# Attention's output products in three 16-bit terms, with low parts made on VectorE, and the second key copy read from 16-bit data

## What is computed

```python
q = (x @ w_q).reshape(b, s, h, -1).transpose(0, 2, 1, 3)
kv = x @ w_kv
...
q = _l2norm(q) * jnp.exp(scale)
k = _l2norm(k)
sim = jnp.einsum('bhid,bhjd->bhij', q, k)
attn = jax.nn.softmax(sim, axis=-1)
out = jnp.einsum('bhij,bhjd->bhid', attn, v)
out = out.transpose(0, 2, 1, 3).reshape(b, s, h * out.shape[-1])
return out @ w_out + b_out
```

## Time and profile before

| | us |
|---|---|
| median of 3 runs (1051.28 to 1055.02) | 1051.43 |
| the profiled execution, its own time | 1044.7 |
| its span, first to last instruction | 1042.9 |
| TensorE busy / VectorE busy / ScalarE busy / GpSimd busy | 911.9 / 732.2 / 768.9 / 503.0 |
| first scores start | 35.0 |
| last output product starts | 631.5 |

### The profile page before, as it was taken

How to read it: one execution, slowest core, us unless ns; L and a number is a source line. 1 busy time by engine, 2 the same in 40 slices (tenths; PEclk the granted TensorE clock), 3 DMA queues, 4 the chain that set the end, 5 groups by cost and what they waited for, 6 DMA issues and landing times. The chain is left out here.

```text
span 1042.9 us, 34710 instructions
## 1 busy us (share of the span) xinstructions
PE 911.9 (87%) x13676; PEld 856.1 (82%) x13676; DVE 732.2 (70%) x1432; ACT 768.9 (74%) x1275; POOL 503.0 (48%) x384
## 2 busy tenths in 40 slices
PE   4789999999999999999999997989969589899930
PEld 2678998998999989888889987989958479899830
DVE  6699989888988988888998974424549769400202
ACT  5689998998988999988889865445465366697831
POOL 5465655555554654644778800323327180052423
PEclk8799999999999999999999998999989689899965
DMA  8400000000000000000001020713111012023111
GB/s 256 130 2 3 23 3 23 2 3 22 3 3 22 3 3 23 3 3 23 9 8 37 13 63 7 231 55 91 45 29 31 1 36 64 16 72 98 57 57 43
DMA packets 43563, 42.13 MB, mean 40 GB/s; under 512 B 5648, under 2 KB 37392, under 8 KB 43408
## 3 DMA queue, kind: packets, MB, share of 16 engines
q1 hardware_dynamic: 39312, 31.51, 10.1%
q0 software_dynamic: 4096, 8.40, 2.6%
HBM read 25.60 MB, written 14.29 MB: 38 GB/s over the span
## 5 line engine op out<-in xcount | busy, mean ns | idle before, releaser
L688 ACT ACTIVATE Pr<-SC,nesc,esc 128x1024 f32<-128x1024 f32 x256 | 310.0, 1211 | 33.2 <-PE SC L505 22.9
L804 DVE TENSOR_TENSOR Pl<-Pr 128x1024 f16<-128x1024 f32 x224 | 293.2, 1326 | 39.7 <-ACT Pr L688 38.1
L504 PE MATMUL SC<-QK 128*128 128x256 f16 x1024 | 238.6, 273 | 1.0 <-ACT QK L670 1.0
L505 PE MATMUL SC<-QK 128*128 128x256 f16 x1024 | 238.6, 273 | 0.0
L530 PE MATMUL OP<-V,Pr 128*128 128x65 f16 x2048 | 214.4, 192 | 6.3 <-DVE Ob L827 6.2
L532 PE MATMUL OP<-V,Pr 128*128 128x64 f16 x2048 | 215.3, 195 | 0.0
L534 PE MATMUL OP<-V,Pl 128*128 128x65 f16 x2048 | 214.1, 191 | 0.0
L530 PEld LDWEIGHTS OP<-V,Pr 128*128 128x128 bf16 x2048 | 191.0, 97 | 13.4 <-issue 9.2
L532 PEld LDWEIGHTS OP<-V,Pr 128*128 128x128 bf16 x2048 | 190.0, 97 | 2.6
L534 PEld LDWEIGHTS OP<-V,Pl 128*128 128x128 f16 x2048 | 190.7, 99 | 0.0
L1055 POOL TENSOR_TENSOR stk<-nrm,stk 128x512 f16<-128x512 f32 x64 | 75.1, 1173 | 139.8 <-DVE stk L786 139.8
(11 more groups left out here) (224 smaller groups left out, 2168.2 us busy)
## 6 DMA issues: line engine op xcount, KB each, us to landing
ys<-yb SPq DMA_DIRECT2D x92, 64.0 KB, 1.5
w_or_rows<-xs SPq DMA_DIRECT2D x12, 384.0 KB, 4.2
wst<-in_up SPq DMA_DIRECT2D x8, 512.0 KB, 3.5
xs<-zero SPq DMA_DIRECT2D x2, 1472.0 KB, 13.4
scratch<-in_up SPq DMA_DIRECT2D x4, 576.0 KB, 4.5
wd<-in_wd SPq DMA_DIRECT2D x4, 576.0 KB, 5.8
wd<-in_wd SPq DMA_DIRECT2D x4, 512.0 KB
QK<-in_wqkv SPq DMA_DIRECT2D x4, 384.0 KB, 7.5
```

The source lines that it names most:

```text
L504: eng.matmul(out, QK[:, b, 1, key:key + P], rhs, start=True, stop=False)
L505: mm = eng.matmul(out, QK[:, b, 2, key:key + P], rhs, start=False, stop=True)
L688: eng.activation(Pr[:, n % PB, :, :], SC[s % 2][:, :, :], ACT.Exp, bias=nesc[:, hd:hd + 1], scale=esc[:, hd:hd + 1]).then_inc(s_exps, 1)
L804: eng.tensor_tensor(Pl[:, n % PB, :, :].rearrange("p a b -> p (a b)"), pr, high(pr)[:, 1::2], ALU.subtract).then_inc(s_low_probs, 1)
```

## The change

It touches the output products, the output weights and the second key copy.

- `out_product` has three 16-bit matmuls instead of one 32-bit: the upper halves of `OT` (read as bf16 in place) with the high and with the low part of the weights, and the low part of `OT` with the high part of the weights. They add up in PSUM. It waits for `s_out_low` instead of `s_out_turned_read`.
- The low part of `OT` is a new subtraction on VectorE, `low_out`, 128 x 256 elements a unit, 64 in all, into a buffer `OTl` of two units. `low_slot` puts it two slots before its product: slots 7, 10, 13, 16, 23, 25, 27 and 29, behind that slot's `low_probs` and ahead of an `add_out` of the same slot. It waits for the copy of `OT` and for the product two units before, whose place in `OTl` it takes.
- The weights are loaded into `OT`'s memory and split once, in slots 16 and 18 of pass 0, on VectorE (`split_out_weights`): a cast to `wo_hi` and a subtraction to `wo_lo`. TensorE's wait for the load is gone; ScalarE's first copy into `OT` waits for the split, and each copy waits for the product of its place one pass before.
- `copy_keys` reads the 16-bit keys that `high_parts` has just written, instead of the 32-bit ones, and so waits for `s_qk_high` of its own group.

```diff
+SPLIT_WO_AT = (16, 18)
...
+def low_slot(u):
+
+    return OUT_AT[u] - 2
...
-        wo = sb("wo", [P, H // 2 * D], F32)
+        wo_hi = sb("wo_hi", [P, H // 2 * D], F16)
+        wo_lo = sb("wo_lo", [P, H // 2 * D], F16)
...
+        OTl = sb("OTl", [P, 2, 2 * P], F16)
+        wo = OT[:, 0:H // 4, :, :].rearrange("p u r c -> p (u r c)")
...
             def out_product(i, u):
 
-                wait(eng, s_out_turned_read, 8 * i + u + 1)
+                wait(eng, s_out_low, 8 * i + u + 1)
                 for r in range(2):
                     pair = (2 * i + u // 4) % TB
-                    mm = eng.matmul(out_bank(i, u)[:, P * r:P * r + P], OT[:, u, r, :],
-                                    wo[:, D * pair:D * pair + D], start=True, stop=True)
+                    out = out_bank(i, u)[:, P * r:P * r + P]
+                    hi, lo = high(OT[:, u, r, :])[:, 1::2], OTl[:, u % 2, P * r:P * r + P]
+                    wh, wl = wo_hi[:, D * pair:D * pair + D], wo_lo[:, D * pair:D * pair + D]
+                    eng.matmul(out, hi, wh, start=True, stop=False)
+                    eng.matmul(out, hi, wl, start=False, stop=False)
+                    mm = eng.matmul(out, lo, wh, start=False, stop=True)
                 mm.then_inc(s_out_product, 1)
...
-            eng.wait_ge(s_loaded["wo"], 16)
             eng.wait_ge(s_squares, PJ)
...
                 wait(eng, s_out_turned, 8 * i + u + 1)
+                if (i, u) == (0, 0):
+                    eng.wait_ge(s_wo_low, 1)
+                wait(eng, s_out_product, 8 * (i - 1) + u + 1)
                 eng.activation(OT[:, u, :, :], M1[:, 0:2 * P].rearrange("p (r c) -> p r c", r=2), ACT.Copy).then_inc(
                     s_out_turned_read, 1)
...
             def copy_keys(h, hb, g):
-                G, b = 4 * h + g, g % 2
+                G = 4 * h + g
                 wait(eng, s_turned, 8 * (h - 1) + 2 * g + 2)
-                eng.tensor_copy(stk[:, g, :, 4 * DH:5 * DH], nrm[:, b, :, 1, :]).then_inc(s_k_copied, 1)
+                wait(eng, s_qk_high, G + 1)
+                eng.tensor_copy(stk[:, g, :, 4 * DH:5 * DH], stk[:, g, :, 2 * DH:3 * DH]).then_inc(s_k_copied, 1)
...
+            def split_out_weights(s):
+
+                if s == SPLIT_WO_AT[0]:
+                    eng.wait_ge(s_loaded["wo"], 16)
+                    eng.tensor_copy(wo_hi[:, :], wo).then_inc(s_wo_high, 1)
+                if s == SPLIT_WO_AT[1]:
+                    eng.wait_ge(s_wo_high, 1)
+                    eng.tensor_tensor(wo_lo[:, :], wo, wo_hi[:, :], ALU.subtract).then_inc(s_wo_low, 1)
+
+            def low_out(i, u):
+
+                wait(eng, s_out_turned_read, 8 * i + u + 1)
+                wait(eng, s_out_product, 8 * i + u - 1)
+                o = OT[:, u, :, :].rearrange("p r c -> p (r c)")
+                eng.tensor_tensor(OTl[:, u % 2, :], o, high(o)[:, 1::2], ALU.subtract).then_inc(s_out_low, 1)
...
+                    split_out_weights(s)
+                if (x := out_unit(s, low_slot)) and exists(i, x[0]):
+                    low_out(i - x[0], x[1])
                 if (x := out_unit(s, out_slot)) and exists(i, x[0]):
```

More of the change, by code:

```diff
@@ L323, in attention @@
         s_k_copied = sem("s_k_copied")
+        s_wo_high = sem("s_wo_high")
+        s_wo_low = sem("s_wo_low")
+        s_out_low = sem("s_out_low")
         s_qk_low = sem("s_qk_low")
@@ L429, in _ @@
                     eng.dma_start(scl[:, :], io["scale"].partition_broadcast(P)).then_inc(s_loaded["scl"], 16)
-            eng.dma_start(wo[:, :], io["wout"]).then_inc(s_loaded["wo"], 16)
+            eng.dma_start(wo, io["wout"]).then_inc(s_loaded["wo"], 16)
             eng.dma_start(t["x"][:, :, :], io["x"].rearrange("(t p) d -> p t d", p=P)).then_inc(s_loaded["x"], 16)
```

## The result

The changed kernel takes **1112.45 us** (median of 4 runs, 1110.78 to 1114.36) against 1052.35 for the kernel before beside it: a ratio of 1.0571, interval 1.0550 to 1.0592. The forecast was 1067 with a range of 1055 to 1079: the sign was right, the size was missed by 45 us. The profiled execution took 1112.4 us, its span 1110.7.

A forecast was written before the change was run, and what follows sets the result against it. TensorE bounds by shares, with VectorE a second bound in slots 4 to 14 and 20 to 30. Passes lose 12.8 us and the tail 3.3, together 16.1, or 1.5% on the median 1051.43: 1067 us, range 1055 to 1079.

The forecast's parts named there:

- the copy should come at 0.04: Key copy on VectorE: starts 0.04 us after the cast ends, ahead of GpSimd's subtraction at 0.08; 0.06 us more per group.
- the rival: Key copy falls behind GpSimd's subtraction and waits 1.2 us, about 52 us on top: 1120 us; chance 0.06.
- TensorE's part: Output products: six 16-bit matmuls take 0.33 us, saving 0.19 us per unit, 0.11 in two units of eight.
- Its rival: TensorE decides and low parts are hidden: seven passes save 1.36 us each, 9.5 in all, 1042 us; chance 0.07.
- The low part: VectorE's 256-element subtraction per unit: 0.41 us until the result, 0.33 in VectorE's queue.
- First half: Pass 3, slots 4 to 20: TensorE waits on low parts, slot 15's product 1.51 us late; half loses 1.13 us.
- Second half: Pass 3: no loss in slot 25, slot 29's product delayed 1.23 us by its addition, savings 0.19 + 0.11; net 0.93 us lost.
- Passes 1 to 4: Attention's passes 1 to 4: each loses 2.06 us, 8.2 together.
- The split: Output weights' cast and subtraction (0.7 and 1.2 us) in pass 0, slots 16 and 18, where VectorE idles: loss taken as 0.
- Pass 5: ScalarE scales eight rows more and bounds more of the first half: half of a pass's loss, 1.2 us.
- The tail: Eight products after the last scores: units 1 to 4 wait for additions, 1.4 us a unit instead of 0.62; 3.3 us lost.
- The free wait: Waiting on the neighbour costs nothing: key copy saves 0.07 us per group instead of losing 0.06, 1061 us; chance 0.15.

The follow-up runs named there:

- with one wait: Changed kernel without the key copy's wait for the turned keys of the head before, leaving only the wait for the cast: 1073.35 us, 1.0192 to before.
- the run with early low parts: Changed kernel with the old 32-bit key copy, low parts of turned outputs taken in slots 0 to 3 and 16 to 19, four buffers: 1064.85 us.
- the best version: Changed kernel with old key copy, four low-part buffers, low parts in slots 0 to 3 and at the ends of slots 18 and 19: 1055.31 us, 1.0032.
- the next run: Old key copy, low parts in slots 0 to 3, 18 and 19, plus the weight split put before pass 0's first exponential: 1057.19 us, 1.0038.

## Why the prediction was wrong, point by point

**The step that failed** is "the copy should come at 0.04". I took the 0.04 from the earlier trace rows, where an instruction's wait for its neighbour stands in the instruction itself. The new wait was written last, became an instruction of its own, and the copy comes at 0.10, in all 60 groups of the slot loop between 0.102 and 0.104; GpSimd comes at 0.08 in 59 of them. With the wait in the copy itself it comes at 0.034, as I had read. 0.02 us decided over 39. The diff showed both waits and their order; I priced the added wait by its neighbour's end and did not ask where it stands.

**The chance.** I had the rival, its place and the two rows that it rested on. 0.06 for it was too little: the lead was 0.04 us, without a row for two waits, and the price 52 us by its own sum.

**The rival's size.** "About 1 us x 4 x 13 = 52 on top": a group holds VectorE 0.81 us longer (2.55 against 1.73 with one wait). Taken for all 60 groups, as pass 0 has them too, that makes 49, of which 39 reached the time. Pass 0, left out there, lost 4.7 of them (76.8 against 72.1).

The Trainium skill has this rule, and I did not weigh it: "SBUF — State Buffer", section "Who interferes with whom", says that VectorE's copies in two-port modes, and its instructions with two inputs from SBUF, share a pair of ports with GpSimd, that whoever issues first holds it for the whole instruction while "the other fully blocks", and that sums along the row take no part in it on this chip. The traces agree: a copy of 0.23 us takes 1.22 and ends 0.08 after GpSimd, a low part of 0.41 takes 1.95 and ends 0.28 after it, and the sum at 280.26 (GpSimd behind the copy) takes 0.68 beside GpSimd's subtraction as without it. In one point the traces are narrower: GpSimd's power of eight elements (1.63 us) does not hold VectorE. In the changed kernel 46 of VectorE's low probabilities run wholly beside it and take 1.19 to 1.23 us, as when GpSimd idles.

**TensorE's part** was right: 0.33 us for the six matmuls (in the run with early low parts a product starts at 285.88 and the next transposes at 286.22). Its rival, that TensorE decides and 9.5 us are saved, did not come about even with the low parts out of the full stretches of VectorE's queue: there 0.3 us a pass show.

**The low part**: 0.41 was right for the median (0.417), not for the mean: 0.52 with one wait, as 14 of 64 take over 0.6. In pass 3 those are the ones of slots 16 and 27 (0.88 and 0.87), which end 0.28 after GpSimd's subtraction for the values.

**First half**, forecast 1.13: with one wait 1.31 (36.69 against 35.38), and TensorE reaches slot 15's product 1.50 us late, where the sum said 1.51. The wait of 0.8 us in slot 12 is 0.6 there, but most of it stands before attention's products (0.43 at 286.04) and only 0.09 before the output product. **Second half**, forecast 0.93: 1.30. In slot 25, "no loss", the product is 0.5 later; in slot 29 it waits 1.29 us instead of 0.27, 1.0 more against the 1.23 worked out. TensorE, with one wait:

```profile
296.20 0.22 PE L565 MATMUL M<-wo_hi,OT 128*128 128x128 f16 x1 [0.57 <-DVE OTl L863]
...
331.08 0.22 PE L565 MATMUL M<-wo_hi,OT 128*128 128x128 f16 x1 [1.29 <-DVE x L870]
```

Passes 1 to 4 come to 10.1 instead of 8.2.

**The split**, "0 to 1, I take 0": pass 0 lost 1.8. The cast that I put at 0.7 us came behind GpSimd's low probabilities (timeline with one wait):

```profile
74.56 2.87 POOL L1070 TENSOR_TENSOR Pl<-Pr 128x1024 f16<-128x1024 f32 x1
...
75.60 2.38 DVE L853 CAST wo_hi<-OT 128x1024 f16<-128x1024 f32 x1
```

**Pass 5**, "half of a pass's loss, 1.2": 3.0. With the low parts moved past GpSimd it loses 1.1, its second half nothing (41.56 against 42.00), so some 2 us of the 3 go back to where low parts stand. **Pass 6** 1.3 instead of 2.1, **pass 7** 0.9 instead of 1.1. **The tail**, 3.3: 3.5 with one wait and 3.8 after. Products follow one another by 1.43 us at first, as worked out, and by 1.73 when the granted clock has fallen to its lower level, 1.2 GHz (0.50 from 646 to 652 us with one wait, 0.99 in the 4 us before). On both sides of that fall TensorE idles 0.94 us before the products that wait for a low part. Two of after's, at the lower clock:

```profile
685.92 0.27 PE L565 MATMUL M<-wo_hi,OT 128*128 128x128 f16 x1 [0.94 <-DVE OTl L864]
687.67 0.27 PE L565 MATMUL SC<-wo_hi,OT 128*128 128x128 f16 x1 [0.94 <-DVE OTl L864]
```

Without the fallen copy the sum of 16.1 stands against 20.5 by the stages and 21 by the medians, and 1073 lies inside the range: the terms that were too small are those where a new instruction came beside GpSimd (the split, pass 5, low parts of 0.88).

**The free wait** (second rival) falls: a copy that doesn't wait starts 0.085 us before its neighbour's end, one that waits 0.034 after it, or 0.103 when the wait stands apart. The Trainium skill's sentence, in "VectorE: DVE Perf Modes", "The DRAIN you can't avoid", that the semaphore costs nothing extra is not borne out here: a group takes 0.04 us more (1.694 to 1.736), although the copy itself is 0.06 shorter.

What stays open: the 0.3% that the best version stays above before was not taken apart further than by the stages of its profile: pass 0 and pass 5 1.0 and 1.1 us longer, the tail 1.0 shorter, passes 1 to 4 0.6 shorter, and pass 7 3.3 longer, with the wait of 1.9 behind the long low probabilities shown above. In the next run's profile these take 2.88 us, and pass 7 is 0.6 longer than before. How often either happens is not known.

## What to carry to other kernels

When two engines are released by the same event and one of them can hold the other, ask which starts first, and where each of its waits stands: the wait that comes last belongs in the instruction itself, and an order that rests on hundredths of a microsecond has to be priced as lost until it is set. Look for free time of an engine only where the engine that can hold it is idle too; for a subtraction, VectorE's gaps beside GpSimd's subtractions were no gaps. And before a shorter instruction is put into a chain, see what ends the chain: here each group ended with GpSimd's subtraction, so that a shorter copy could win nothing.

## What the runs showed of the hardware

- Of two waits in front of a VectorE instruction one is an instruction of its own. If that is the one for the neighbour, the start comes 0.069 us later (0.103 against 0.034 after the neighbour's end); if it is the other, nothing is lost. GpSimd starts 0.079 us after the same event.
- An instruction of VectorE that comes after GpSimd's has started shows no idle time in the trace but a longer duration: the copy 1.22 us instead of 0.23, the 32-bit copy 1.21 instead of 0.29, a low part up to 2.72 instead of 0.41, the maximum of eight elements 0.41 to 0.64 instead of 0.17. A long mean of a short instruction is how such a hold is read.
- A hold can outlast one instruction: low probabilities that came 0.12 us after GpSimd's took 5.34 us instead of 1.22, through three instructions of GpSimd.
- It goes the other way too: in pass 0 of the run with one wait GpSimd's low probabilities, started 0.15 us after VectorE's (74.41, 1.27 us), took 2.87 us instead of 1.90.
